# Slot attention: queries read from PSUM, two of eight score products on GpSimd, a second buffer of values, rounds written out

## The reference, cut to what matters

```python
x = x + 0.5 * moe(layernorm(x))          # moe_a
x = x + linear_attention(layernorm(x))   # linatt
x = x + 0.5 * moe(layernorm(x))          # moe_b
x = x + 0.5 * fp4_ffn(layernorm(x))      # ffn_a
x = x + slot_attention(layernorm(x))     # att: the one that is changed
x = x + 0.5 * fp4_ffn(layernorm(x))      # ffn_b
```

```python
lin = einsum('sbe,fe->sbf', query, in_proj_weight) + in_proj_bias   # s = 8 slots, b = 512
q, k, v = split(lin.reshape(8, 512 * 16, 3, 8))                     # 16 heads of 8
attn = softmax(einsum('sbd,tbd->bst', q, k) * 8 ** -0.5)
ctx = einsum('bst,tbd->sbd', attn, v).reshape(8, 512, 128)
out = einsum('sbe,fe->sbf', ctx, out_proj_weight) + out_proj_bias
```

## Time and profile before

| | |
|---|---|
| median of 3 runs | 740.05 us (737.7 to 740.06) |
| the profiled execution's own time | 742.46 us |
| its span, first to last instruction | 740.5 us |
| mean granted TensorE clock | 0.971 of full speed |
| busy: PE, DVE, ACT, POOL | 666.4, 605.3, 458.3, 295.1 us |

### The profile page before, as it was taken

How to read it: one execution, slowest core, us unless ns; L and a number is a source line. 1 busy time by engine, 2 the same in 40 slices (tenths; PEclk the granted TensorE clock), 3 DMA queues, 4 the chain that set the end, 5 groups by cost and what they waited for, 6 DMA issues and landing times.

```text
span 740.5 us, 16304 instructions
## 1 busy us (share of the span) xinstructions
PE 666.4 (90%) x5826; PEld 478.0 (65%) x5826; DVE 605.3 (82%) x1554; ACT 458.3 (62%) x867; POOL 295.1 (40%) x417
## 2 busy tenths in 40 slices
PE   4999999979999999999996789999979978889995
PEld 2777776658788776777774556566647546556564
DVE  2688878746767688978786899999999999899983
ACT  3777777775576338777785476657544434576642
POOL 5000022056556501010013677554535538677520
PEclk9999999999999999999999799999999999999997
DMA  8000000000000000000000000000000000010100
GB/s 210 23 0 0 0 1 0 2 2 4 3 0 3 3 2 1 1 1 0 0 1 0 1 0 1 1 0 1 2 0 0 0 1 1 0 29 15 29 15 28
DMA packets 13463, 7.10 MB, mean 10 GB/s; under 512 B 1177, under 2 KB 13409, under 8 KB 13409
## 3 DMA queue, kind: packets, MB, share of 16 engines
q1 hardware_dynamic: 11328, 5.33, 2.7%
q10 hardware_dynamic: 2080, 1.05, 0.5%
HBM read 4.28 MB, written 2.10 MB: 9 GB/s over the span
## 4 chain that ended last, share of the span: by engine, by line
PE 64%; DVE 16%; ACT 10%; issue 6%; POOL 3%; DMA 1%; DVEq 0%; POOLq 0%; ACTq 0%
PE ps L1464 59%; DVE shared L1275 3%; DVE shared L1303 3%; PE ps L1859 2%; DVE x_sb L1100 2%; ACT ffn_work L536 2%; ACT ffn_work L737 2%; PE ps L1472 1%; ACT xnT L587 1%; ACT x_sb L846 1%; PE ps L1478 1%; ACT ffn_work L574 1%; DVE stats L1001 1%; ACT hqT L842 1%; ACT ffn_work L569 1%
## 5 line engine op out<-in xcount | busy, mean ns | idle before, releaser
L1464 PEld LDWEIGHTS ps<-w_sb,sq_h 128*128 128x128 f32 x1024 | 133.1, 193 | 71.1 <-ACT sq_h L606 51.0
L1100 DVE SCALAR_TENSOR_TENSOR x_sb<-ps,gates,x_sb 128x128 f32 (+1 forms) x512 | 147.0, 343 | 21.4 <-PE ps L1464 17.3
L1464 PE MATMUL ps<-w_sb,sq_h 128*128 128x128 f32 x1024 | 138.8, 279 | 3.3 <-ACT sq_h L606 3.3
L1464 PE MATMUL ps<-xnT,w_sb 128*128 128x512 f32 x256 | 134.9, 610 | 0.0
L602 ACT ACTIVATE relu_h<-ps 128x512 f32<-128x512 f32 x128 | 75.6, 590 | 57.8 <-PE ps L1464 57.5
L357 POOL TENSOR_SCALAR vareps<-meanvar 128x4 f32<-128x4 f32 (+1 forms) x28 | 8.9, 319 | 255.7 <-DVE meanvar L1010 255.3
L606 ACT ACTIVATE sq_h<-relu_h 128x512 f32<-128x512 f32 x128 | 80.6, 630 | 4.0
L1464 PE MATMUL ps<-gateT,xnT 128*128 128x352 f32 x128 | 58.9, 544 | 17.4 <-ACT ffn_work L737 13.0
L404 POOL TENSOR_TENSOR shared<-shared 128x128 f32<-128x128 f32 x112 | 51.5, 459 | 27.2 <-ACT shared L696 19.0
L580 ACT ACTIVATE xn<-x_sb,shift,rstd 128x128 f32 (+1 forms) x136 | 57.1, 481 | 6.5 <-POOL shift L365 5.6
L1464 PE MATMUL ps<-downT,hqT 128*128 128x128 f32 x384 | 57.4, 288 | 4.2 <-ACT hqT L842 4.0
(11 more groups left out here) (166 smaller groups left out, 1335.7 us busy)
## 6 DMA issues: line engine op xcount, KB each, us to landing
x_sb<-in_L_attn_x_dram SPq DMA_DIRECT2D x8, 256.0 KB, 7.1
out_dram<-x_sb SPq DMA_DIRECT2D x8, 256.0 KB, 2.3
w_sb<-in_L_ffn_w_all_dram ACTq DMA_DIRECT2D x2, 512.0 KB, 6.3
wraw<-in_L_attn_qkv_w_dram SPq DMA_DIRECT2D x1, 192.0 KB, 4.8
wraw<-attn_in_proj_weight_dram SPq DMA_DIRECT2D x1, 192.0 KB, 3.7
fraw<-in_L_ffn_w_down_dram SPq DMA_DIRECT2D x1, 176.0 KB, 3.1
fraw<-in_L_ffn_w_gate_dram SPq DMA_DIRECT2D x1, 128.0 KB, 2.7
fraw<-in_L_ffn_w_up_dram SPq DMA_DIRECT2D x1, 128.0 KB, 2.5
```

The lines of the kernel that those rows point to most:

```text
L1100: t = nc.vector.scalar_tensor_tensor(tile_b(i, j), bank(4 + e % 4, TPB, C)[:, j, :], gates[:, j, e:e + 1], tile_b(i, j), ALU.mult, ALU.add)
L1464: return nc.tensor.matmul(o, a, b, start=start, stop=stop, **kw)
```

## The change

Four things, all in the attention phase:

1. **Queries stay in PSUM.** `make_q` writes them to banks 2 and 3 as the last of the three projections, and no copy to SBUF is made for slots 0 to 5. `qk` becomes one `scalar_tensor_tensor` that reads the query from PSUM, adds the bias (a column of `in_b_col`) and multiplies by `kT`.
2. **Two of eight products go to POOL.** DVE makes slots 0 to 5 (`DQ = 6`). ACT copies the queries of slots 6 and 7 to `q_late` (`take_late_q`), and `late_products` on POOL multiplies them, behind `slot_pairs`. `score(i, 1)` waits for both (`qk_ready`, `qk_late`).
3. **Values are double-buffered** (`v_att[:, i % 2]`) and made before the queries, from banks 2 and 3 (banks 4 and 5 in the first round). ACT copies them right after `exp_half(i, 1)`, ahead of the normalisation of round i+2.
4. **The rounds are written out** on all four engines, without a hardware loop. With it, half of the layer-norm sums of round i+2 stand ahead of `less_max(i, 0)` on DVE in rounds 0 and 1, and on ACT `x_out(i, 0)` stands ahead of `ctx_half(i, 1)`.

```diff
-        qT = part(0, 1024, "p (b t) -> p b t", b=B)
-        kT = part(1024, 1024, "p (b t) -> p b t", b=B)
-        v_att = part(2048, 1024, "p (b f) -> p b f", b=B)
+        v_att = part(0, 2048, "p (s b f) -> p s b f", s=2, b=B)
+        kT = part(2048, 1024, "p (b t) -> p b t", b=B)
+        q_late = sb("q_late", [P, B - DQ, P])
...
+            def late_products(i):
+
+                s = S["att"]
+                pool.wait_ge(s["lin_ready"], 5 * i + 5 if i > 0 else 3)
+                for b in range(DQ, B):
+                    pool.wait_ge(s["ctx_done"], B * i + b + 1)
+                    nc.gpsimd.tensor_tensor(prod[:, b, :, :], kT[:, :, :],
+                                            q_late[:, b - DQ, :].unsqueeze(1).to_broadcast([P, B, P]),
+                                            ALU.mult).then_inc(s["qk_late"], 1)
...
-                    with pool.Fori(0, TPB - 2) as i:
+                    late_products(0)
+                    for i in range(TPB - 2):
                         ln_group(s, i + 2, B)
                         slot_pairs(s, i)
+                        late_products(i + 1)
                     ffn_b.layer_norm(0)
                     slot_pairs(s, TPB - 2)
+                    late_products(TPB - 1)
                     ffn_b.x_divide(0)
...
                 def take_v(self, i):
-                    self.take(i, 4, v_att, None)
-                    self.take(i, 5, v_att, None)
+                    for n in range(2):
+                        act.wait_ge(self.s["lin_done"], 6 * i + n + (3 if i > 0 else 5))
+                        nc.scalar.activation(v_att[:, i % 2, 4 * n:4 * n + 4, :], bank(v_bank(i) + n, 4, P),
+                                             ACT.Copy).then_inc(self.s["lin_ready"], 1)
+
+                def take_late_q(self, i):
+                    act.wait_ge(self.s["lin_done"], 6 * i + (6 if i > 0 else 4))
+                    nc.scalar.activation(q_late[:, :, :], bank(3, 4, P)[:, DQ - 4:4, :], ACT.Identity,
+                                         bias=in_b_col[:, 0:1]).then_inc(self.s["lin_ready"], 1)
...
                     exp_half(i, 1)
+                    if more:
+                        front.take_v(i + 1)
                     if ahead2:
                         ahead(i + 2)
...
                     ctx_half(i, 0)
+                    if more:
+                        front.take_late_q(i + 1)
+                    x_out(i, 0)
                     ctx_half(i, 1)
-                    if more:
-                        front.take_v(i + 1)
-                    x_out(i, 0)
                     x_out(i, 1)
...
                     dve.wait_ge(s["ctx_done"], B * i + b + 1)
-                    nc.vector.tensor_tensor(prod[:, b, :, :], kT[:, :, :],
-                                            qT[:, b, :].unsqueeze(1).to_broadcast([P, B, P]),
-                                            ALU.mult).then_inc(s["qk_ready"], 1)
+                    nc.vector.scalar_tensor_tensor(prod[:, b, :, :],
+                                                   bank(2 + b // 4, 4, P)[:, b % 4, :].unsqueeze(1).to_broadcast([P, B, P]),
+                                                   in_b_col[:, 0:1], kT[:, :, :],
+                                                   ALU.add, ALU.mult).then_inc(s["qk_ready"], 1)
...
                 def body(i, more, ahead2):
+                    if ahead2:
+                        ln_sums(ch, i + 2, range(B // 2), tile_t)
                     less_max(i, 0)
                     if ahead2:
+                        ln_sums(ch, i + 2, range(B // 2, B), tile_t)
 
                         dve.wait_ge(s["xn_ready"], i + 2)
-                        ln_stats(s, ch, i + 2, B, tile_t)
+                        ln_moments(s, ch, B)
...
                 def score(self, i, k):
 
 
-                    pe.wait_ge(self.s["qk_ready"], B * i + 4 * k + 4)
+                    pe.wait_ge(self.s["qk_ready"], DQ * i + min(4 * k + 4, DQ))
+                    if k == 1:
+                        pe.wait_ge(self.s["qk_late"], (B - DQ) * (i + 1))
...
                     if more:
-                        front.make_qk(i + 1)
+                        front.make_k(i + 1)
                     bias_out(i, more)
+                    if more:
+                        front.make_v(i + 1)
                     for b in range(4):
                         context(i, b)
...
                     if more:
-                        front.make_v(i + 1)
+                        front.make_q(i + 1)
                     project_out(i, 0)
...
+DQ = 6
```

More of the change, by code:

```diff
@@ L832, in last_body @@
                     x_out(i, 1)
-                with act.Fori(0, TPB - 2) as i:
+                for i in range(TPB - 2):
                     body(i, True, True)
@@ L1849, in att @@
                 pe.wait_ge(S["ffn_a"]["x_done"], GROUPS)
-                with pe.Fori(0, TPB - 1) as i:
+                for i in range(TPB - 1):
                     body(i, True)
@@ L1936, in _ @@
             ffn(S["ffn_b"], False, None)
[L1940 removed]
+PER = {"moe": 17, "linatt": 4}
+DQ = 6
 GATES = 4
```

82 lines of the change are left out of this document (40 added, 42 removed).

## The result

The changed kernel takes 735.21 us (median of 6 runs, 733.63 to 736.13) against 740.28 us for the kernel before, measured beside it (6 runs, 737.7 to 745.42). The ratio of the runs is 0.9899 with a 95% interval from 0.9877 to 0.9922: 7.5 us faster, 5.8 to 9.1.

A forecast was written before the change was run, and what follows sets the result against it. DVE was taken to set the pace of the attention, with PE nearly as long and the bound after the change. Savings of 2.5, 3.0 and 1.9 made 7.4, taken as 7.0: 740.05 - 7.0 = 733.0 us, range 730.5 to 737.5.

The forecast's parts named there:

- DVE, P to L: From a round's last `pv` (P) to the next round's first maximum (L): DVE alone needs 8.0 us, before 10.55.
- PE: PE's work in a round, 20.4 us, plus a tail chain of 5.2: 25.6 us a round, more than DVE's 25.2.
- POOL to `context` 7: Last pair sum, undisturbed at 1.27 us, ends 1.7 after the last `pv`; `context` 7 ends 2.9 after it.
- The added products: Two 1024-element products on POOL at 2.36 us each; they cost nothing while under 3.0 us each.
- Loops: No pause at the loop's edge on the engines, so writing out the rounds changes nothing.
- ACT: One short query copy replaces two; value copies may delay the normalisation by some 1.2 us; effect on the time nothing.
- Three rounds: Attention rounds 0, 1 and 2 save 2.5, 3.0 and 1.9 us, together 7.4.
- From 7.4 to 7.0: Three chains end within half a microsecond in each round, handoffs cost a few hundredths each; 7.0 us taken.
- half clock: Rival: PE's clock drops in the attention rounds, each drop costing 1.4 to 1.6 us; 734.5 to 737.5 us; chance 0.12.
- POOL was not late: Rival: POOL products take 4 us each, shifting the maxima of rounds 2 and 3 by 1.9 each; 737 us; chance 0.07.
- The contention that stays: Rival: bias column counts as second SBUF input, DVE and POOL work go in turn; 9 us slower, 749; chance 0.06.
- The late queries: Rival: moved `make_q` or value copies are late, DVE waits at the last `pv`; gain under 3.7 us; chance 0.05.

The follow-up runs named there:

- e6: The changed kernel with one of the two output-bias matmuls of each round made twice on PE; 737.94 us, ratio 0.9931 to the kernel before.
- e7: The changed kernel with all eight extra layer-norm sums behind the first maximum, as before the change; 734.12 us, ratio 0.9895 to the kernel before.
- e2: The changed kernel with all eight queries copied to SBUF, so DVE and POOL both read two SBUF tensors; 761.13 us, ratio 1.0234 to the kernel before.
- e1: The changed kernel with all eight products on DVE, none on POOL, queries still in PSUM; 738.17 us, ratio 0.9946 to the kernel before.
- e3: The kernel before with its attention rounds written out on all four engines and nothing else; 742.16 us, ratio 1.0002 to the kernel before.
- e4: The changed kernel with three products on POOL instead of two (`DQ = 5`); 734.23 us, ratio 0.9908 to the kernel before.

## Why the prediction was right

It was 733.0 us, 7.0 less than before, in a range of 730.5 to 737.5. Measured are 735.21 and a ratio that makes 7.5 us. The number that the trace bears out is that of the phase, 8.08 us against a sum of 7.4 (7.31 before its terms were rounded). Step by step:

- **DVE, P to L.** `qk` at 1.27 instead of the forecast 1.31, pitch 1.19 instead of 1.20. In round 0 DVE was ready at 545.06 - 0.23 = 544.83, P + 8.02; the step said P + 8.0. A slip stands in it: the half of the sums that goes ahead was charged to every round, but it stands only before the maxima of rounds 0 and 1, so at the end of round 1 DVE was ready at 570.40 - 1.01 = 569.39, P + 7.24. It cost the forecast nothing, since PE was later in both; it is why DVE's pauses were 1.01 and 1.10 where 0.3 to 1 stood, and only 0.23 in round 0.
- **PE.** Forecast 20.4 + 5.2 = 25.6 a round; measured 20.18 + 5.16 = 25.34. The way to the last 32 context records took 16.68 us in the round of before from which the step read it and takes 16.44 now; 0.18 of that lies in the matmuls of keys and queries, 3.72 together before and 1.82 + 1.72 now (why was not tested). The tail was added up from durations of rows that overlap by 0.07. Rounds 1 and 2 came out 0.26 and 0.33 under 25.6, and the maximum of round 1 came 0.18 earlier behind `ffn_a`'s last copy than forecast; these 0.77 are what the 8.08 have over 7.31. That added work on PE would now count was right (e6), but the bound did not pass to PE alone. The step put `context` 7 behind the pair sum 0.3 us inside PE's own time (L + 20.1 against L + 20.4); it is 0.02 (P + 2.96 against P + 2.98), and DVE's work from L to P counts as much (e7).
- **POOL to `context` 7.** Pair sum at P + 1.75 (forecast P + 1.7), context 7 at P + 2.98 (P + 2.9). The contention went from both sides, as L1197 had suggested; e2 shows what the same split costs with it. One of the 32 pair sums took 1.72, in round 3 beside a product of `ffn_b` with both inputs in SBUF, as in the kernel before.
- **The added products.** 2.358 to 2.388 us each (forecast 2.36), from P + 2.23 to P + 6.93 (P + 2.3 to P + 7.0), 1.2 to spare (forecast 1.4, from P + 7.0 to P + 8.4). The extrapolation from 128 and 512 elements to 1024 held within 0.03, though its stated ends did not follow: half and twice the rate give 1.8 and 3.5 us, not 1.9 and 4.7. e1 gives their worth: 4.8 us of the phase.
- **Loops.** Nothing, as e3 shows by itself. **ACT.** DVE never waited for queries, and the only ACT pauses on PE are the two copies of the tail.
- **Three rounds.** First maxima at 519.74, 545.06, 570.40 and 595.67, where 519.5, 545, 570.6 and 596 were said.
- **From 7.4 to 7.0, and the range.** The 0.4 taken off for handoffs between the chains has no row behind it, and the phase shows no such loss: it gave more than 7.4. That 7.0 lies close to the 7.5 of the ratio is in part luck: a term that was too long on PE and a deduction without a row both made the forecast smaller, and the interval of the ratio, 5.8 to 9.1, can't tell 7.0 from 8.1. The lower end of the range took a round of 24.8 from DVE alone, although the same working puts PE's round at 25.6, so a round of 24.8 was not open.

Of the rivals, half clock did not come: the granted clock is 1.00 in the windows of all three rounds, and PE was idle for 1.9, 1.5 and 1.5 us in them. The mechanism is real all the same, since in e2 a pause of 4.56 us was followed by 3.44 for a row of 1.92, at a granted clock of 0.56. POOL was not late with two products and a little late with three (e4). The contention that stays did not come, so the bias column does not count as a second SBUF input; but with both inputs in SBUF (e2) a phase became 99.24, and the sign of the whole change hangs on this one operand. The late queries did not come.

The last step, from the profiled execution to the median, was the weakest: the sum was set against a median of three runs, 740.05, and the median of the kernel before alone moved by 3.6 us from one series to another (740.28, 741.84, 742.46, 742.52, 743.9). Both runs of the change gave the ratio 0.9899, while their medians were 5.1 and 7.8 us below those of before.

## What to carry to other kernels

Before splitting elementwise work over DVE and POOL, look at where each operand lies: with one operand of VectorE in PSUM the two engines ran side by side, and the same split with both in SBUF was slower than no split at all. An engine that is slower at an operation (2.36 us against 1.21 here) is still the right place for it when it is idle in that stretch and the result is due later than it needs; the due time, read from the trace, says how many fit (two here, not three). When several chains end within a tenth of a microsecond of each other, shortening one gives next to nothing, and an experiment that lengthens each in turn or shortens them together is what tells the tie from a single bound.

## What the runs showed of the hardware

Two products that both read two SBUF tensors took 3.36 and 3.32 us for 1.21 and 2.36, so each engine paid nearly the other's full time, more than the 2.27 for 1.27 of the earlier trace rows had shown. Small POOL instructions are caught too: in e2 a 128x8 `tensor_tensor` beside the first `qk` took 1.19 us, against 0.20 at the same place of the changed kernel, beside the `qk` that read PSUM.

```profile
513.02 1.19 POOL L369 TENSOR_TENSOR shift<-negmean,rstd 128x8 f32<-128x8 f32 x1
```

```profile
510.25 0.20 POOL L369 TENSOR_TENSOR shift<-negmean,rstd 128x8 f32<-128x8 f32 x1
```

The first of these two rows is from e2, the second from the changed kernel. The form with the bias column, in contrast, takes a little more time itself (1.273 against the plain 1.21 for 1024 elements) but costs POOL none, whose products took 2.36 to 2.39 beside it.
